# A fused attention layer on one core: conversions in pairs, key pages loaded sooner, 2 KB stores, and ScalarE's order and scans

## The chip, the core and the metric

One NeuronCore of a Trainium2 chip runs the whole program. TensorE (PE) multiplies and transposes, VectorE (DVE), ScalarE (ACT) and GpSimd (POOL) do the element work, and SyncE (SP) does nothing but issue transfers. The metric is the device time of one execution in microseconds (us). Less is better.

## What is computed

The input x is 32 x 32 x 512: 32 sequences of 32 tokens with 512 features. A first layer adds to each sequence a product with a 32 x 32 matrix that is picked by an index. The second is attention with 32 query heads and 8 key heads of 128 elements, whose keys and values are partly new and partly in a cache of 64 pages of 32 tokens:

```python
x = x + einsum('bct,bcd->bdt', x, L0_weights[subjects])
q, k, v = x @ Wq.T, x @ Wk.T, x @ Wv.T            # 32, 8 and 8 heads of 128
q, k = rope(rmsnorm(q) * q_norm, pos), rope(rmsnorm(k) * k_norm, pos)
k_all = concat([k_cache[block_table], k]); v_all = concat([v_cache[block_table], v])
scores = where(valid, einsum('bqhd,bkhd->bhqk', q, repeat(k_all, 4)) * SCALE, -1e30)
out = x + einsum('bqhk,bkhd->bqhd', softmax(scores), repeat(v_all, 4)) @ Wo.T
```

## The kernel before

**Two stages.** The first is a loop over 96 *units* (`for u in range(NU)`, one such loop in each engine's program). A unit is one of 12 *chunks* of 512 columns of the projection weights (8 of the queries in units 0 to 63, 2 of the keys in 64 to 79, 2 of the values in 80 to 95) times one of 8 groups of 128 tokens. The second is a loop over 256 *steps* (`for i in range(STEPS)`), one for each sequence and key head: scores, softmax, weighting of the values, and in the later steps the output projection of earlier groups (`ps_y`). Each number is held as two parts, a high and a low one, so that three products stand for one.

**A unit.** PE makes 12 products into `ps_proj` and then turns the rotated heads of the unit three before it (`ps_rt<-fixed,roped`, L1707). ACT squares the 512 columns, writes the high part of the turned heads (`stage`, L1125) and of the next chunk's weights (`wt_hi`). DVE rotates (`rot`, L1395 for queries, L1403 for keys, four instructions), writes the low part of the turned heads (`stage`, L1413) and, in four of eight units, the low part of the next weights (`wt_lo`). POOL adds the two halves (`roped`). SP stores the turned heads to `q_t` or `k_new_t` in DRAM.

**What holds PE back in this loop.** PE may be three units ahead, since `ps_proj` has three buffers. Its transposes at the end of unit u wait for `v_rtlo`, which is DVE's L1413 of the unit five before, and DVE does that one in its own unit u-2:

```python
un = u - LAG
...
if un >= 2:
    pe.wait_ge(v_rtlo, un - 1)
```

**The tasks.** Beside the projections 84 *tasks* go over the cache pages and the weights, 0.5 MB each: 52 *scans* (largest magnitude; ACT L1137, or DVE L1423 when `scan_on_dve`) and 32 *conversions* (ACT L1145 writes the high part, then DVE L1427 the low part, then SP stores the two as `k_pages_t` or `v_pages`). `TASKS` is their fixed order, `TASK_IN[u]` says which are done in unit u: before, two in each of units 1 to 6 and one in each unit from 7 to 78. A task's data go through one of four buffers `c_nat`: SP loads task t+4 (`load_c`, L682) after it has seen task t done. The scales for the conversions come from the scans: `reduce_tops` at units `K_BOUND` and `V_BOUND`, with PE's and DVE's small steps three and six units later.

**Keys and queries for the steps.** For each sequence SP loads 16 key pages into `kt` (L719), the queries into `qt` (L706) and the new keys (L708). The pages of sequence 0 go out in units 54 to 69, those of sequence 1 from `NEXT_KEYS_AT` on, one a unit; later ones during the steps.

**A step on ACT and DVE.** ACT writes the high part of the turned probabilities (`t_hi`, L1043) and DVE the low part (`t_lo`, L1285). Once in four steps ACT also takes the context out of `ps_o` (`ot_hi_of`, L1073), and DVE its low part (`ot_lo`, L1302). From step 24 on, in just those steps, DVE does `t_lo` first of all (`late_new`).

Of the kernel before, what the change touches and what calls it, by code (L numbers as in the profile page):

```python
# [9 lines left out]
F16 = mybir.dt.float16  # L10
# [8 lines left out]
B, SEQ, HID = 32, 32, 512  # L19
D, HQ, HK = 128, 32, 8  # L20
# [9 lines left out]
GB = P // SEQ  # L30
# [29 lines left out]
def build(nc, x, rows_in, table, l0_w, wq_t, wk_t, wv_t, wo_t, norms_in, kc_t, v_cache, wv,  # L60
# [23 lines left out]
    k_pages_t = nc.dram_tensor("k_pages_t", (PAGES, D, NHALF * BLK), F16).ap()  # L84
    k_new_t = nc.dram_tensor("k_new_t", (B, D, NHALF * BLK), F16).ap()
    q_t = nc.dram_tensor("q_t", (B, D, HK * BLK), F16).ap()

# [198 lines left out]
    XSUM_BOUND = float(np.sqrt(HID)) * (1.0 + 2.0**-10)  # L286
    KEYS_AT, NEXT_KEYS_AT, PREFETCH, NEW_V_AT = 54, 80, 87, 93
    WO_LOADS = {84: 0, 86: 1, 88: 2}
# [4 lines left out]
    TOP_STEP = 3  # L293
    K_BOUND, V_BOUND, W_BOUND = 11, 47, 80

    def mixed(convs, scans):
# [3 lines left out]
        for i in range(n):  # L300
# [3 lines left out]
            else:  # L304
# [6 lines left out]
             + [("scan", n) for n in WO_SCANS[:7]] + mixed(V_CONVS, WO_SCANS[7:]))  # L311
    PAIRS = 6
    TASK_AT = 1
    TASK_OF = {what: t for t, what in enumerate(TASKS)}
    TASK_IN = {u: [] for u in range(NU)}
    for t in range(len(TASKS)):
        TASK_IN[TASK_AT + t // 2 if t < 2 * PAIRS else TASK_AT + t - PAIRS].append(t)

    def scan_on_dve(n):
        return n % 3 == 2  # L320

    def scanned(eng, n):

        if scan_on_dve(n):
            eng.wait_ge(v_scan, n // 3 + 1)
        else:
            eng.wait_ge(a_scan, n - n // 3 + 1)

# [14 lines left out]
    def wo_scanned(eng):  # L343
        eng.wait_ge(a_scan, NSCAN - NSCAN // 3)
        eng.wait_ge(v_scan, NSCAN // 3)

# [303 lines left out]
    with persist, nc.Block() as block:  # L650
        @block.sync
        def _(sp):
# [48 lines left out]
            def load_queries(b):  # L701

                s = b % 2
                if b >= 2:
                    sp.wait_ge(t_qk, HK * (b - 1))
                sp.dma_start(qt[s][:].rearrange("p j f -> p (j f)"), q_t[b]).then_inc(d_qt[s], 16)  # L706
                edge = kt[s][:].rearrange("p (a f) -> p a f", f=BLK)[:, 0:2 * NPP + 2:2 * NPP + 1, :]
                sp.dma_start(edge, k_new_t[b].rearrange("d (h f) -> d h f", h=NHALF)).then_inc(d_kt[s], 16)  # L708

# [25 lines left out]
            for u in range(NU):  # L735
# [6 lines left out]
                if LAG < u <= NN + LAG:  # L742
                    un = u - LAG - 1
                    cn, gn = units[un]
                    kind, _, k = chunks[cn]
                    sp.wait_ge(v_rtlo, un + 1)
                    at_k = k if kind == "q" else NHALF - 1 - k
                    dst = (q_t if kind == "q" else k_new_t)[GB * gn:GB * (gn + 1), :, at_k * BLK:(at_k + 1) * BLK]
                    sp.dma_start(dst.rearrange("b d f -> d b f"), stage[un % NST][:].rearrange("p (b f) -> p b f", b=GB)
                                 ).then_inc(d_st[un % NST], 16)  # L750
# [35 lines left out]
                if NEXT_KEYS_AT <= u < NEXT_KEYS_AT + NPP:  # L786
                    load_pages(1, u - NEXT_KEYS_AT, 1)
                if u in WO_LOADS:
# [210 lines left out]
        def _(act):  # L999
# [798 lines left out]
```

## Time and profile before

| | before |
|---|---|
| median of 3 executions | 999.94 us (999.54 to 1003.92) |
| the profiled execution | 1002.31 us, of which the span is 1000.5 us |
| PE busy | 960.5 us, 96% |
| DVE busy | 831.1 us, 83% |
| ACT busy | 754.4 us, 75% |
| POOL busy | 579.8 us, 58% |

The span is from the first to the last instruction of the profiled execution; 1.8 us of its time lie outside. The busy shares are means over two stages that have little in common, so the stretches are read one by one below: 54 to 304 us hold the units 7 to 80, 304 to 341 us the rest of the units up to the first scores, and 341 to 967 us the steps.

### The profile page before, as it was taken

What the parts mean: (1) busy time and instruction counts of PE and PEld (TensorE: products, weight loads), DVE (VectorE), ACT (ScalarE), POOL (GpSimd) and SP (SyncE); (2) the same over time, 40 slices, a digit from 0 to 9 for tenths busy, and PEclk for the clock granted to TensorE, in tenths of its full rate; (3) what the DMA queues carried; (4) which work ended last, traced back from release to release, by engine and by line L of the source; (5) the groups of instructions that cost most, each with busy time, mean ns of one, the idle gap of its engine ahead of it and who ended that gap; (6) DMA issues with size and microseconds to landing.
All of it is one profiled execution on the core that took longest, in us unless ns stands there. A gap on an engine that the chain in (4) does not pass through costs nothing.

```text
span 1000.5 us, 25118 instructions
## 1 busy us (share of the span) xinstructions
PE 960.5 (96%) x8075; PEld 797.7 (80%) x8075; DVE 831.1 (83%) x1844; ACT 754.4 (75%) x2104; POOL 579.8 (58%) x861
## 2 busy tenths in 40 slices
PE   6899999999899999899999999999999999999998
PEld 4578888887677787788888888888888888878885
DVE  7889999999997688888878878888887887878880
ACT  5898999988784688878777777777777777767760
POOL 5565665565893067666755655565566556655550
PEclk9999999999999999999999999999999999999999
DMA  5899999989998999999999999999999999999940
GB/s 196 298 318 323 330 383 370 384 276 389 391 335 270 337 310 360 337 290 272 292 316 269 289 310 284 278 301 280 314 259 288 335 260 276 316 296 258 264 128 11
DMA packets 249907, 294.92 MB, mean 295 GB/s; under 512 B 79024, under 2 KB 206512, under 8 KB 247216
## 3 DMA queue, kind: packets, MB, share of 16 engines
q1 hardware_dynamic: 231088, 226.07, 76.5%
q0 software_dynamic: 18688, 67.25, 18.1%
q8 instruction: 65, 1.06, 0.4%
q14 instruction: 66, 0.54, 0.2%
HBM read 231.77 MB, written 46.27 MB: 278 GB/s over the span
## 4 chain that ended last, share of the span: by engine, by line
PE 74%; DVE 12%; issue 4%; ACT 3%; DMA 3%; POOL 2%; SPq 1%; DVEq 0%; ACTq 0%; POOLq 0%
PE ps_proj L1531 17%; PE ps_y L1531 16%; PE ps_o L1612 14%; PE ps_s L1569 8%; PE ps_t L1583 7%; PE ps_s L1573 7%; PE ps_rt L1707 2%; DVE probs L1265 2%; DVE rot L1403 2%; DVE c_stage L1427 2%; DVE stage L1413 1%; PE ps_o L1624 1%; DVE wt_lo L1231 1%; DVE rot L1395 1%; DMA c_nat<-in_L_cond_k_cache 1%
## 5 line engine op out<-in xcount | busy, mean ns | idle before, releaser
L1037 ACT ACTIVATE probs<-probs,neg_max 128x544 f32<-128x544 f32 x256 | 191.7, 749 | 137.8 <-DVE neg_max L1265 130.5
L1265 DVE CUSTOM_DVE_ANT_0 probs<-ps_s,mask,row_scale 128x544 f32<-128x544 f32 x256 | 200.4, 783 | 51.4 <-PE ps_s L1573 42.9
L1612 PE MATMUL ps_o<-pt,vs 128*128 128x128 f16 x3072 | 213.9, 219 | 0.9 <-DMA vs<-v_pages,v_row 0.9
L1612 PEld LDWEIGHTS ps_o<-pt,vs 128*128 128x128 f16 x3072 | 193.3, 98 | 15.7 <-DMA vs<-v_pages,v_row 1.5
L961 POOL TENSOR_SCALAR probs<-probs,recip 128x512 f32<-128x512 f32 x144 | 99.8, 693 | 170.1 <-DVE recip L1273 167.5
L907 POOL TENSOR_TENSOR roped<-rot 128x256 f32<-128x256 f32 x160 | 144.9, 927 | 81.3 <-DVE rot L1395 76.1
L1531 PE MATMUL ps_proj<-wt_hi,x0t_hi 128*128 128x512 f32 x384 | 158.6, 414 | 6.5 <-DVE x0t_lo L1221 6.0
L1285 DVE SCALAR_TENSOR_TENSOR pt<-ps_t,pt 128x512 f16<-128x512 f32 x190 | 130.3, 686 | 41.5 <-ACT pt L1043 41.3
L1531 PE MATMUL ps_y<-wo,ot_hi 128*128 128x512 f16 x512 | 153.4, 381 | 2.4 <-DVE ot_lo L1302 2.4
L1531 PE MATMUL ps_proj<-wt_hi,x0t_lo 128*128 128x512 f32 x384 | 150.3, 393 | 0.0
L1531 PE MATMUL ps_proj<-wt_lo,x0t_hi 128*128 128x512 f32 x384 | 149.3, 390 | 0.0
L942 POOL DMA_INDIRECT vs<-v_pages,v_row x128 | 130.8, 1022 | 27.7 <-issue 12.3
L1569 PE MATMUL ps_s<-kt,qt 128*128 128x256 f16 (+1 forms) x768 | 136.6, 287 | 1.7 <-DMA kt<-k_pages_t 1.7
L1573 PE MATMUL ps_s<-kt,qt 128*128 128x288 f16 (+1 forms) x768 | 126.2, 273 | 3.5 <-DVE neg_max L1265 3.2
L1583 PE MATMUL ps_t<-fixed,probs 128*128 128x128 f32 x760 | 115.1, 274 | 5.1 <-POOL probs L961 2.4
L1043 ACT ACTIVATE pt<-ps_t 128x512 f16<-128x512 f32 x190 | 111.6, 587 | 9.2 <-PE ps_t L1583 7.3
L1583 PEld LDWEIGHTS ps_t<-fixed,probs 128*128 128x128 f32 x760 | 92.2, 141 | 32.1 <-POOL probs L955 4.5
L1112 ACT ACTIVATE squares<-ps_proj 128x128 bf16<-128x128 f32 x320 | 85.2, 296 | 24.8 <-PE ps_proj L1531 24.8
L1531 PE MATMUL ps_y<-wo,ot_lo 128*128 128x512 f16 x256 | 97.0, 379 | 0.0
L1573 PEld LDWEIGHTS ps_s<-kt,qt 128*128 128x128 f16 x768 | 74.0, 98 | 22.7 <-DVE neg_max L1265 7.4
L1531 PEld LDWEIGHTS ps_proj<-wt_hi,x0t_hi 128*128 128x128 f32 x384 | 72.2, 188 | 21.4 <-DVE x0t_lo L1221 8.2
L955 POOL TENSOR_SCALAR probs<-probs,recip 128x544 f32<-128x544 f32 (+1 forms) x64 | 43.2, 674 | 77.5 <-DVE recip L1273 75.6
(162 smaller groups left out, 1809.7 us busy)
## 6 DMA issues: line engine op xcount, KB each, us to landing
kt<-k_pages_t SPq DMA_DIRECT2D x512, 128.0 KB
c_nat<-in_L_cond_k_cache SPq DMA_DIRECT2D x32, 512.0 KB, 6.2
q_t<-stage SPq DMA_DIRECT2D x64, 256.0 KB, 7.0
c_nat<-in_L_cond_v_cache SPq DMA_DIRECT2D x32, 512.0 KB, 7.0
qt<-q_t SPq DMA_DIRECT2D x32, 512.0 KB, 3.3
w_nat<-in_L_cond_Wq SPq DMA_DIRECT2D x8, 1024.0 KB, 8.0
k_pages_t<-c_stage SPq DMA_DIRECT2D x16, 512.0 KB, 5.3
c_nat<-in_L_cond_Wo SPq DMA_DIRECT2D x16, 512.0 KB, 7.0
```

The lines of the kernel that those rows point to most:

```text
L907: last = pool.tensor_tensor(dst, a, b, ALU.add)
L942: pool.indirect_dma_start(vs[b % 2][:, c].rearrange("p j s d -> p (j s d)"), None, v_pages, bass.IndirectOffsetOnAxis(ap=v_row[:, b * NCH ...
L961: pool.tensor_scalar(old_keys(i), old_keys(i), col(recip, i), 1.0, ALU.mult, ALU.mult).then_inc(p_old, 1)
L1037: act.activation(pr, pr, ACT.Exp, bias=col(neg_max, i), scale=-1.0, accum_out=col(row_sum, i)).then_inc(a_exp, 1)
L1043: act.activation(pt_part(i, 0), t_bank("t", i)[:], ACT.Copy, scale=P_SCALE).then_inc(a_thi, 1)
L1265: dve.tensor_tensor_reduce(out=probs_of(i), in0=ps_s[:, score_cols(i):score_cols(i) + KEYS], in1=mask[(i // HK) % 2][:, mask_at(i):mask_at ...
L1285: dve.scalar_tensor_tensor(pt_part(i, 1), t_bank("t", i)[:], P_SCALE, pt_part(i, 0), ALU.mult, ALU.subtract).then_inc(v_tlo, 1)
L1531: ins = pe.matmul(ps, a, b, start=first and n == 0, stop=last and n == len(pairs) - 1)
L1569: pe.matmul(own[0], q[:, a], k[:, b, own[1]:own[2]], start=n2 == 0, stop=n2 == 2)
L1573: ins = pe.matmul(shared[0], q[:, a], k[:, b, shared[1]:shared[2]], start=n2 == 0, stop=n2 == 2)
L1583: ins = pe.transpose(t_bank("t", i)[:, c * P:(c + 1) * P], probs_of(i)[:, SEQ * (i % 2) + c * P:SEQ * (i % 2) + (c + 1) * P], ident[:])
L1612: ins = pe.matmul(ps_o[n % 2][:, jl * P:(jl + 1) * P], v[:, part, :], pt[pt_slot(i)][:, NCH * half + c, :], start=jl == 1 and c == 0 and k ...
```

## The change

Six edits, made together:

- `q_t` and `k_new_t` are laid out by group of four sequences. A unit's store is now one run of 2048 bytes in each partition where it was four of 512. The query load, which was one run of 4096 bytes, becomes eight of 512.
- Units 18, 26, 34 and 42 do two tasks each, so that every task after them comes one unit sooner for each such unit passed, and four units sooner from unit 42 on. The last task is done in unit 74 and was done in unit 78. `V_BOUND` moves from 47 to 43.
- The last two scans that DVE had (numbers 47 and 50) go to ACT.
- The key pages of sequence 1 are loaded from unit 76 on, was 80, pages 2 to 15 first and then 0 and 1, behind a wait for `v_proj` of unit 79.
- In a step ACT does `ot_hi_of` after `t_hi`, not ahead of it.
- The waits that count scans are adapted.

```diff
-    k_new_t = nc.dram_tensor("k_new_t", (B, D, NHALF * BLK), F16).ap()
-    q_t = nc.dram_tensor("q_t", (B, D, HK * BLK), F16).ap()
+    k_new_t = nc.dram_tensor("k_new_t", (NG, D, NHALF, GB * BLK), F16).ap()
+    q_t = nc.dram_tensor("q_t", (NG, D, HK, GB * BLK), F16).ap()
...
-    KEYS_AT, NEXT_KEYS_AT, PREFETCH, NEW_V_AT = 54, 80, 87, 93
+    KEYS_AT, NEXT_KEYS_AT, PREFETCH, NEW_V_AT = 54, 76, 87, 93
-    K_BOUND, V_BOUND, W_BOUND = 11, 47, 80
+    K_BOUND, V_BOUND, W_BOUND = 11, 43, 80
-    PAIRS = 6
-    TASK_AT = 1
+    PAIR_UNITS = (1, 2, 3, 4, 5, 6, 18, 26, 34, 42)
+    TASK_UNITS = [u for u in range(1, NU) for _ in range(2 if u in PAIR_UNITS else 1)]
     for t in range(len(TASKS)):
-        TASK_IN[TASK_AT + t // 2 if t < 2 * PAIRS else TASK_AT + t - PAIRS].append(t)
+        TASK_IN[TASK_UNITS[t]].append(t)
+
+    SCAN_SPLIT = NSCAN - 6
     def scan_on_dve(n):
-        return n % 3 == 2
+        return n % 3 == 2 and n < SCAN_SPLIT
...
-                sp.dma_start(qt[s][:].rearrange("p j f -> p (j f)"), q_t[b]).then_inc(d_qt[s], 16)
+                g, a = divmod(b, GB)
+                mine = slice(a * BLK, (a + 1) * BLK)
+                sp.dma_start(qt[s][:], q_t[g, :, :, mine]).then_inc(d_qt[s], 16)
...
-                    dst = (q_t if kind == "q" else k_new_t)[GB * gn:GB * (gn + 1), :, at_k * BLK:(at_k + 1) * BLK]
-                    sp.dma_start(dst.rearrange("b d f -> d b f"), stage[un % NST][:].rearrange("p (b f) -> p b f", b=GB)
+                    sp.dma_start((q_t if kind == "q" else k_new_t)[gn, :, at_k], stage[un % NST][:]
...
-                    load_pages(1, u - NEXT_KEYS_AT, 1)
+                    pg = (u - NEXT_KEYS_AT + 2) % NPP
+                    if pg == 0:
+                        sp.wait_ge(v_proj, NN)
+                    load_pages(1, pg, 1)
...
             for i in range(STEPS):
-                if at(i, OE) is not None:
-                    ot_hi_of(at(i, OE))
                 if at(i, TNE) is not None:
                     tn_hi(at(i, TNE))
                 if i < NP2 and not by_dma(i):
                     t_hi(i)
+                if at(i, OE) is not None:
+                    ot_hi_of(at(i, OE))
```

Three places in the order of the instructions. On DVE, units 74 to 77, near the end of the key chunks (`c_stage` is a conversion, `abs_sums` a scan, `rot` and `stage` the unit's own work) stood, before:

```order
L1403 SCALAR_TENSOR_TENSOR rot<-ps_proj,rstd,rope_k 128x2x128 x4
L1413 TENSOR_TENSOR stage<-ps_rt,stage 128x4x128
L1231 TENSOR_TENSOR wt_lo<-w_nat,wt_hi 128x4x128
L1427 SCALAR_TENSOR_TENSOR c_stage<-c_nat,scale,c_stage 128x8x128
L1403 SCALAR_TENSOR_TENSOR rot<-ps_proj,rstd,rope_k 128x2x128 x4
L1413 TENSOR_TENSOR stage<-ps_rt,stage 128x4x128
L1231 TENSOR_TENSOR wt_lo<-w_nat,wt_hi 128x4x128
L1423 TENSOR_REDUCE abs_sums<-c_nat 128x1
```

and in the changed kernel in units 74 and 75, as in 76 and 77 (its lines are numbered six higher):

```order
L1409 SCALAR_TENSOR_TENSOR rot<-ps_proj,rstd,rope_k 128x2x128 x4
L1419 TENSOR_TENSOR stage<-ps_rt,stage 128x4x128
L1237 TENSOR_TENSOR wt_lo<-w_nat,wt_hi 128x4x128
L1409 SCALAR_TENSOR_TENSOR rot<-ps_proj,rstd,rope_k 128x2x128 x4
L1419 TENSOR_TENSOR stage<-ps_rt,stage 128x4x128
```

So the conversions and the scan are gone from these units. The first piece shows units 75 and 76.

On DVE in units 18 and 19, at the first of the four doubled units, the changed kernel has:

```order
L1401 TENSOR_TENSOR rot<-ps_proj,rope_q 128x1024
L1419 TENSOR_TENSOR stage<-ps_rt,stage 128x4x128
L1233 SCALAR_TENSOR_TENSOR wt_lo<-w_nat,w_inv,wt_hi 128x4x128
L1433 SCALAR_TENSOR_TENSOR c_stage<-c_nat,scale,c_stage 128x8x128 x2
L1401 TENSOR_TENSOR rot<-ps_proj,rope_q 128x1024
L1419 TENSOR_TENSOR stage<-ps_rt,stage 128x4x128
L1233 SCALAR_TENSOR_TENSOR wt_lo<-w_nat,w_inv,wt_hi 128x4x128
L1429 TENSOR_REDUCE abs_sums<-c_nat 128x1
```

Before, unit 18 had one conversion, unit 19 the other, and the scan came in unit 20.

On ACT, in a step that takes the context out, before:

```order
L1037 ACTIVATE probs,row_sum<-probs,neg_max 128x544
L1073 ACTIVATE ot_hi<-ps_o 128x32x16
L1043 ACTIVATE pt<-ps_t 128x512
L1037 ACTIVATE probs,row_sum<-probs,neg_max 128x544
L1060 ACTIVATE ptn<-ps_t 32x256 x2
```

and in the changed kernel:

```order
L1043 ACTIVATE probs,row_sum<-probs,neg_max 128x544
L1049 ACTIVATE pt<-ps_t 128x512
L1079 ACTIVATE ot_hi<-ps_o 128x32x16
L1043 ACTIVATE probs,row_sum<-probs,neg_max 128x544
L1066 ACTIVATE ptn<-ps_t 32x256 x2
```

The high part of the turned probabilities (`pt`) now goes ahead of that of the context (`ot_hi`).

## Rows read from the trace of the kernel before

**Rows 1.** Busy time by stretch; (x) is the number of instructions.

```profile
core 0: us, PE busy (x) PEld busy (x) DVE busy (x) ACT busy (x) POOL busy (x), PEclk, DMA share, GB/s
57.60:239.80 182.20, 182.03 (x916) 150.11 (x915) 174.23 (x215) 164.19 (x642) 109.14 (x130) 1.00 1.00 350
239.80:275.00 35.20, 30.80 (x149) 23.68 (x148) 33.08 (x53) 26.50 (x106) 28.66 (x35) 1.00 1.05 392
275.00:303.70 28.70, 25.97 (x127) 20.55 (x126) 28.07 (x50) 21.20 (x77) 25.68 (x32) 1.00 0.89 316
340.90:412.40 71.50, 64.52 (x679) 54.44 (x679) 61.10 (x155) 59.02 (x131) 41.31 (x53) 1.00 0.98 321
412.40:950.00 537.60, 530.92 (x5468) 451.38 (x5467) 440.02 (x1184) 404.22 (x944) 322.06 (x530) 1.00 1.02 289
```

**Rows 2.** Chain that ended last, 303 to 312 us: start, us, what.

```profile
303.99 2.77 PE ps_proj L1531 x12
306.76 0.44 PE ps_rt L1707 x4
```

**Rows 3.** PE's waits, 239.8 to 303.7 us: us in total, times, longest.

```profile
PE ps_rt L1707 <- DVE stage L1413: 6.6, 8, 1.1
```

**Rows 4.** DVE in time order; first rotations of the key units 64, 73, 74, 75, 78.

```profile
248.02 1.66 DVE L1403 SCALAR_TENSOR_TENSOR rot<-ps_proj,rstd,rope_k 128x256 f32<-128x256 f32 x4 [2.12 <-ACT squares L1112]
...
277.35 1.65 DVE L1403 SCALAR_TENSOR_TENSOR rot<-ps_proj,rstd,rope_k 128x256 f32<-128x256 f32 x4
...
283.58 1.66 DVE L1403 SCALAR_TENSOR_TENSOR rot<-ps_proj,rstd,rope_k 128x256 f32<-128x256 f32 x4 [0.63 <-POOL rstd L931]
...
286.36 1.28 DVE L1427 SCALAR_TENSOR_TENSOR c_stage<-c_nat,scale,c_stage 128x1024 f16<-128x1024 f32 x1
287.55 1.65 DVE L1403 SCALAR_TENSOR_TENSOR rot<-ps_proj,rstd,rope_k 128x256 f32<-128x256 f32 x4
...
295.25 1.21 DVE L1423 TENSOR_REDUCE abs_sums<-c_nat 128x1 f32<-128x1024 f32 x1
...
300.96 1.65 DVE L1403 SCALAR_TENSOR_TENSOR rot<-ps_proj,rstd,rope_k 128x256 f32<-128x256 f32 x4
302.53 0.68 DVE L1413 TENSOR_TENSOR stage<-ps_rt,stage 128x512 f16<-128x512 f32 x1
```

**Rows 5.** DVE in time order; rotations of the query units 61, 62 and 63.

```profile
236.89 1.21 DVE L1395 TENSOR_TENSOR rot<-ps_proj,rope_q 128x1024 f32<-128x1024 f32 x1
...
241.06 1.21 DVE L1395 TENSOR_TENSOR rot<-ps_proj,rope_q 128x1024 f32<-128x1024 f32 x1
...
242.79 1.21 DVE L1395 TENSOR_TENSOR rot<-ps_proj,rope_q 128x1024 f32<-128x1024 f32 x1
```

**Rows 6.** SP's load of task 33 (conversion 6), and ACT's use of it.

```profile
118.47 0.62 SPq L682 DMA_DIRECT2D c_nat<-in_L_cond_k_cache  x1
...
129.00 1.17 ACT L1145 ACTIVATE c_stage<-c_nat,scale 128x1024 f16<-128x1024 f32 x1
```

**Rows 7.** Transfers of task loads (57 to 304 us) and conversions on DVE: ns min/median/max.

```profile
L1427 DVE SCALAR_TENSOR_TENSOR c_stage<-c_nat,scale,c_stage x32: 1267/1749/1776, 97.4 to 299.3; 128x1024 f16<-128x1024 f32 x32
...
DMA to landing us min/median/max: 3.6/6.7/11.6
```

**Rows 8.** Waits, 412.4 to 950 us: us in total, times, longest.

```profile
DVE pt L1285 <- ACT pt L1043: 38.2, 57, 2.3
...
PE ps_y L1531 <- DVE ot_lo L1302: 1.7, 6, 0.3
```

**Rows 9.** The first key load that PE waited for in the steps.

```profile
376.86 0.50 PE L1569 MATMUL ps_s<-kt,qt 128*128 128x256 f16 x3 [0.93 <-DMA kt<-k_pages_t]
```

More of the change, by code:

```diff
@@ L326, in scanned @@
         else:
-            eng.wait_ge(a_scan, n - n // 3 + 1)
+            eng.wait_ge(a_scan, n - min(n, SCAN_SPLIT) // 3 + 1)
     NQ = NG * HK
@@ L343, in wo_scanned @@
     def wo_scanned(eng):
-        eng.wait_ge(a_scan, NSCAN - NSCAN // 3)
-        eng.wait_ge(v_scan, NSCAN // 3)
+        eng.wait_ge(a_scan, NSCAN - SCAN_SPLIT // 3)
+        eng.wait_ge(v_scan, SCAN_SPLIT // 3)
     TOPS = {K_BOUND: (0, ((0, 0, NKCH),), k_scanned),
@@ L705, in load_queries @@
                     sp.wait_ge(t_qk, HK * (b - 1))
-                sp.dma_start(qt[s][:].rearrange("p j f -> p (j f)"), q_t[b]).then_inc(d_qt[s], 16)
+                g, a = divmod(b, GB)
+                mine = slice(a * BLK, (a + 1) * BLK)
+                sp.dma_start(qt[s][:], q_t[g, :, :, mine]).then_inc(d_qt[s], 16)
                 edge = kt[s][:].rearrange("p (a f) -> p a f", f=BLK)[:, 0:2 * NPP + 2:2 * NPP + 1, :]
-                sp.dma_start(edge, k_new_t[b].rearrange("d (h f) -> d h f", h=NHALF)).then_inc(d_kt[s], 16)
+                sp.dma_start(edge, k_new_t[g, :, :, mine]).then_inc(d_kt[s], 16)
             def load_pages(b, first, count):
```

## The prediction

> **What bounds the kernel now.** I read the busy time by stretch first [rows 1]. In 57.6 to 239.8 us, units 8 to 63, PE is busy for 182.03 of 182.20 us, so that nothing can be won there and only something lost. In 239.8 to 303.7 us (units 64 to 80, the key chunks) PE is busy for 30.80 + 25.97 = 56.77 of 63.90 us: 7.1 us of idle time, 4.4 in the first part and 2.7 in the second, while DVE has 33.08 and 28.07 of them, 96%. In the first steps, 340.9 to 412.4 us, PE idles for 7.0 us. In the steps from 412.4 to 950 us it idles for 6.7 of 537.6, and that is more than half of the kernel with no more than that to give. So the change has some 7 us to win in the key units and a few in the first steps; everywhere else it can only lose.
>
> The chain gives PE's own pace: 2.76 us of products and 0.44 us of transposes, 3.20 us a unit [rows 2]. In 239.8 to 275 us PE issues 149 instructions, at 16 a unit 9.3 units, whose own pace is 29.8 us: 5.4 lost. In 275 to 303.7 it is 127, 7.9 units, 25.4 us: 3.3 lost [rows 1]. Who holds PE is told by its waits: eight transposes waited for DVE's L1413, 6.6 us in all and 1.1 at most [rows 3]. That is the rule of the code: DVE may start its unit at most two units of PE, 6.4 us, less its own rotation and L1413 after PE's products. Those two take 1.73 us for queries (241.06 to 242.79) [rows 5] and 2.25 for keys (300.96 to 303.21) [rows 4], so that the *lag* of DVE behind PE may be 4.7 us in a query unit and 4.2 in a key unit. Beyond that PE stalls for the rest.
>
> **The change part by part.** The ledger of the lag: each unit adds what DVE does in it and takes 3.20 away.
>
> *The second half of the key units.* DVE runs from 283.58 to 300.96 us without a pause, 17.38 us for units 74 to 77, or 4.35 each [rows 4]. The lag grows by 4 x 1.15 = 4.6 us and PE loses the 3.3 us of this part. The change takes from these four units the conversions of 74, 75 and 77 (1.2 us as 286.36 to 287.55, up to 1.7) [rows 4, 7] and the scan of 76 (295.25 to the next rotation, 1.1): 1.2 + 1.7 + 1.1 + 1.7 = 5.7. Left are 11.7 us, 2.9 a unit, under 3.20: the lag shrinks, and no stall is left. Unit 73 gets a conversion (1.2), which leaves the lag near 3.5, still allowed. **-3.3 us** (bounds 2.7, the idle time alone, and 3.5). ACT takes the two scans at 1.1 us each (ACT is busy for 47.7 of 63.9 us there [rows 1]), which hides them.
>
> *The first half.* Units 64 to 72 take DVE 277.35 - 248.02 = 29.3 us up to unit 73, against 9 x 3.2 = 28.8 for PE, but it comes in late: rot of unit 64 waited 2.12 us more [rows 4], at the change from query to key units, where the rotation needs a factor that POOL makes after its additions. Before, these units hold six conversions and one scan; after, six conversions. It saves 1.1, and in exchange the lag at its start is greater, since units 60 to 62 hold two conversions where they held two, but from a higher start. I take 0.8 of the 5.4 as saved. **-0.8 us.** Bounds: 0 and 2.5.
>
> *The doubled units and what follows.* A conversion beside `wt_lo` makes a query unit 4.17 us long (236.89 to 241.06) [rows 5]. A second one adds 1.27 to 1.75 [rows 7], so unit 18 comes to 5.5 to 5.9 us and puts 2.3 to 2.7 on the lag at one stroke. The lag starts from 1.2 there, and the units 19 to 21 (3.6, 4.2, 2.5 us) carry it to about 4.8: a stall of 0.2 to 0.6. The same sum at 26, 34 and 42 peaks at 4.2, 4.1 and 3.3 (0 to 0.2 us of stall). In units 49 to 53 the key tables (two instructions in each of units 49 and 50) now meet conversions 16 to 18, which began at unit 54 before: peak 5.3, stalls of 0.1 and 0.6. Units 60 to 62 give 0.2. Together **+1.4 us**; bounds 0.5 and 2.5. DVE's pauses in this stretch were 182.20 - 174.23 = 8.0 us [rows 1], and the two conversions that move in cost 3.4, so it holds on average.
>
> *Less time for the loads.* A load goes out when the task four before is done. Task 33 was loaded at 118.47 and used at 129.00 us, 10.5 us later [rows 6]; it is now the second of unit 26, with three units instead of four between, so 7.3 us. The median landing is 6.7, the longest 11.6 [rows 7]. This holds for four tasks at each of the four places: ACT will wait for some, 0 to 2 us. What hides it is DVE's own lag of 3 to 4 us just there. At nothing; if the cover fails, it is the slower rival below.
>
> *The stores.* 80 stores go from 512 to 128 runs, 32 query loads from 128 to 1024: 30,720 fewer and 28,672 more. In the units this helps the landings that the last paragraph is about; in the steps it puts the query load, which goes ahead of the pages, up to 0.4 us behind. PE waited 0.93 us for pages of sequence 2 [rows 9]. Nearest rows say +0 to +1 us, I take **+0.5**.
>
> *ACT's order in the steps.* DVE waited 38.2 us for ACT's `pt`, 57 times, 0.67 each [rows 8]. With `t_hi` first, L1285 comes up to 0.5 us sooner in the step where DVE has it first. But PE is busy for 530.92 of 537.6 us whatever DVE does, and of its 6.7 only the 1.7 that it waited for `ot_lo` [rows 8] lie near. `ot_lo` comes later on DVE than masked_max, so that `ot_hi` 0.5 us later is covered. Before step 24 DVE does `ot_lo` ahead of `t_lo`, and there up to 0.5 us in five steps can be lost. **-0.5 us**, bounds -2 and +2.
>
> *Key pages sooner, `V_BOUND`, SP's waits.* Pages of sequence 1 are wanted only when the eight heads of sequence 0 are through; nothing waits for them. The wait for `v_proj` of unit 79 at unit 90 is long met; behind it on SP stand stores of v. SP's wait for all conversions moves to unit 76, three units after the last, and may hold SP for some 4 us; behind it are stores from eight buffers, which have eight units of 3.2 us. Nothing.
>
> **The sum.** -3.3 - 0.8 + 1.4 + 0.5 - 0.5 = -2.7 us. The profiled execution took 1002.31 us (span 1000.5 and 1.8 around it): 999.6. It lies 2.4 above the median of 999.94, and I take that distance as it is: **997.2 us**.
>
> **A rule against it.** In 239.8 to 275 us the transfers moved 392 GB/s [rows 1]. The change brings four loads of 0.5 MB and two stores into the stretch up to 239.8: 182.2 us x 350 GB/s = 63.8 MB become 66.9. At 392 GB/s that needs 171 us, so there is room. The Trainium skill, page "DMA: Bandwidth & Descriptors", section "Specifications", gives some 358 GB/s as the limit of one core at its memory; by that the 66.9 MB would need 187 us, an estimate of 4.7 us more for the stretch. The trace does not agree: 392 stood for 35 us.
>
> **The rivals.**
> - *Less is saved than is lost in the doubled units* (no change). If second conversions cost 1.75, the lag enters unit 64 a microsecond higher, and the first half gives 1 us back: -3.3 + 2.5 + 1 + 0.5 - 0.5 = +0.2, about 1000 us. For it: DVE is at 96% from unit 8 on. Against: the ledger of before gives 8 us of stalls, near what is there.
> - *DVE catches up entirely* (faster). All 7.1 us of the key units go, and ACT's order wins 1 to 2 in the steps: 999.94 - 8.5 = 991.5 us. For it: the scans leave DVE and the lag allowed is nearly met in several places. Against it: the pause at unit 64 stays.
> - *The loads come late* (slower). Its place is the doubled units: if landings rise above 7.3 us under the denser transfers, ACT waits, its squares are late and DVE's lag passes 4.7. If no more than the 350 GB/s of this stretch can be had, 66.9 MB take 191 us, 8.9 more: 999.94 + 8.9 - 2.7 = 1006 us. It decides from landings of about 9 us on (7.3 and what the lag covers). For it: the median is 6.7 and the longest 11.6 us. Against: 392 GB/s were moved, and the stores have fewer runs.
>
> **The numbers.** A measurement of this kernel tells about 0.5%, 5 us, from no change, whose bounds are 994.9 and 1004.9. Forecast 0.52 (994.5 to 999.5), no change 0.19, catching up 0.19, late loads 0.10. Faster by over 0.5%: the third and a part of the first, 0.24. Slower: the last and little else, 0.11. The rest, 0.65, is within. Range 990 to 1003 us: it takes in the first three and leaves out the last.
>
> **What would show it.** Right: in units 74 to 80 no transpose waits for L1413; PE's idle time in the key units falls from 7.1 to about 3.5, in the first half alone; up to unit 63 it rises from 0.2 to 1 or 2, at units 20 to 23 and 51 to 56; the steps' length stays. Wrong: ACT's waits for `c_nat` in the units 26 to 48, or a step loop that is shorter by more than 2 us, or waits for `kt` in it.

## The result, and the profile after

The changed kernel takes 1005.9 us (median of 22 executions, 999.8 to 1010.0) where the kernel before took 1001.4 in executions on the same chips (22, 999.5 to 1004.1). The ratio is 1.0034, with a 95% interval of 1.0021 to 1.0047: by the ratio some 3.4 us slower (the two medians lie 4.5 apart), on the other side of the forecast. The profiled execution took 1007.41 us, with a span of 1005.6.

The busy time by stretch, the same stretches of the program as in [rows 1], with the same columns:

```profile
core 0: us, PE busy (x) PEld busy (x) DVE busy (x) ACT busy (x) POOL busy (x), PEclk, DMA share, GB/s
58.30:250.40 192.10, 186.59 (x918) 150.88 (x916) 178.21 (x218) 168.24 (x648) 108.67 (x130) 0.99 0.96 350
250.40:287.10 36.70, 33.22 (x161) 26.07 (x161) 33.22 (x55) 28.97 (x111) 31.25 (x39) 1.00 1.03 404
287.10:313.20 26.10, 25.77 (x131) 21.09 (x129) 24.06 (x50) 16.73 (x73) 22.63 (x32) 1.00 0.64 224
347.10:419.70 72.60, 64.42 (x679) 54.37 (x679) 61.06 (x155) 59.13 (x131) 40.91 (x53) 1.00 0.97 311
419.70:954.60 534.90, 528.66 (x5463) 449.82 (x5462) 439.63 (x1183) 408.32 (x944) 321.42 (x529) 1.00 1.04 292
```

Units 8 to 63 took 182.2 us and now take 192.1. That is the whole loss and more. Behind it the key units and the later steps are a little faster, and the first steps took 1.1 us longer. Every kernel below is read in such stretches, so here they are for all of them, worked out from the trace: from the start of PE's first product of unit 7 to that of unit 64, and so on, and then from the first scores of step 0 to those of steps 32 and 248 (us, one profiled execution each; "rest" is from unit 82 to the first scores).

| kernel | 7 to 64 | 64 to 74 | 74 to 82 | rest | steps 0 to 32 | 32 to 248 |
|---|---|---|---|---|---|---|
| before | 185.4 | 38.0 | 29.1 | 34.0 | 71.5 | 537.0 |
| changed | 195.3 | 36.7 | 26.1 | 34.0 | 72.6 | 534.8 |
| e1, changed, five buffers | 189.0 | 36.7 | 26.1 | 34.0 | 72.1 | 534.6 |
| e2, changed, no doubled units | 185.4 | 35.9 | 28.4 | 33.9 | 72.1 | 534.9 |
| e3, before, doubled units | 192.1 | 37.6 | 27.2 | 34.0 | 70.6 | 536.9 |
| e4, before, five buffers | 185.5 | 37.8 | 29.2 | 34.0 | 71.1 | 537.3 |
| e5, before, 2 KB layouts | 185.4 | 38.0 | 29.2 | 34.0 | 74.2 | 535.8 |
| e6, before, ScalarE's order | 185.7 | 37.9 | 29.3 | 34.0 | 73.4 | 533.1 |
| e7, other doubled units, five | 189.5 | 36.8 | 25.6 | 34.0 | 72.3 | 534.4 |
| e8, the same with four | 193.1 | 38.6 | 25.6 | 34.0 | 72.6 | 534.3 |
| e9, order, four scans | 185.4 | 35.9 | 29.3 | 34.0 | 70.7 | 534.1 |
| e10, two scans | 185.5 | 37.0 | 28.3 | 34.0 | 71.8 | 537.3 |
| e11, doubled units later, five | 187.1 | 37.2 | 25.6 | 34.0 | 71.8 | 534.8 |
| e12, the best | 187.2 | 36.2 | 25.6 | 34.0 | 72.1 | 534.6 |

What the last two columns hold by chance of one execution: the granted clock fell to one half for 3.4 us at 395 us in e5 and at 397 in e6, in the first steps, and at 889 to 897 us in before, e1, e3, e4, e7, e8, e10, e11 and e12, where the steps 225 and 226 together take 1.1 to 1.4 us more than in the other five. In the changed kernel and e2 step 37 takes 1.3 and 1.5 us more than in before, with a wait of PE for values (`vs`).

**The loss.** Waits of the changed kernel in 58.3 to 250.4 us (us in total, times, longest):

```profile
DVE rot L1401 <- ACT squares L1118: 12.5, 14, 1.9
...
ACT c_nat L1143 <- DMA c_nat<-in_L_cond_Wo: 3.8, 2, 3.6
PE ps_rt L1713 <- DVE stage L1419: 3.0, 7, 0.8
...
PE ps_l L1558 <- ACT angle L1011: 2.4, 2, 1.6
ACT c_nat L1143 <- DMA c_nat<-in_L_cond_v_cache: 1.5, 1, 1.5
```

DVE's wait for ACT's squares was 6.2 us (8 times) before and is 12.5 (14 times). ACT waits for task data, in two large pieces. And PE waits in two ways, of which the prediction knew only one. The time line shows how the pieces hang together (start, duration, what; in brackets the idle time before it and what ended it):

```profile
117.04 0.56 SPq L665 DMA_DIRECT2D w_nat<-in_L_cond_Wq  x1
...
119.61 0.86 SPq L684 DMA_DIRECT2D c_nat<-in_L_cond_v_cache  x1
...
129.08 1.06 ACT L1143 ACTIVATE c_nat<-c_nat 128x1024 f32<-128x1024 f32 x1 [1.50 <-DMA c_nat<-in_L_cond_v_cache]
...
131.29 1.22 DVE L1401 TENSOR_TENSOR rot<-ps_proj,rope_q 128x1024 f32<-128x1024 f32 x1 [1.01 <-ACT squares L1118]
...
138.84 1.23 DVE L1401 TENSOR_TENSOR rot<-ps_proj,rope_q 128x1024 f32<-128x1024 f32 x1 [0.79 <-ACT squares L1118]
...
143.12 0.39 PE L1558 MATMUL ps_l<-w_sq,ones_p 128*128 128x4 f32 x2 [1.56 <-ACT angle L1011]
...
145.07 0.63 PE L1537 MATMUL ps_proj<-wt_hi,x0t_hi 128*128 128x512 f32 x1
...
176.40 0.64 SPq L684 DMA_DIRECT2D c_nat<-in_L_cond_Wo  x1
...
186.02 1.06 ACT L1143 ACTIVATE c_nat<-c_nat 128x1024 f32<-128x1024 f32 x1 [3.56 <-DMA c_nat<-in_L_cond_Wo]
...
199.03 0.39 PE L1558 MATMUL ps_l<-w_sq,ones_p 128*128 128x4 f32 x2 [0.80 <-ACT angle L1011]
```

Unit 27 is the first behind a doubled one. Its task (34) was loaded at 119.61 us, 2.57 us behind the load of the next weights (`w_nat`, 1 MB), and landed 9.5 us later. ACT wanted it 8.0 us after the issue and stood for 1.50. ACT has no slack to work that off in the units 28 and 29, since it makes the next weights there; in the units 29 to 31 it stays 3.2 to 3.7 us behind PE, DVE waits for its squares again and again, and DVE's lag goes to 5.5 us. At unit 32 PE stands for 1.56 us for something that the prediction doesn't name: `ps_l`, the sum of the squared weights of the next chunk, which ACT makes beside the weights (L1011). The same happens behind the doubled unit 42: task 52 was loaded at 176.40, landed 9.6 us later and cost ACT 3.56; PE stood at `ps_l` for 0.80 at unit 48.

Not all that PE lost there was waiting. The granted clock (the column before the last two):

```profile
141.60:144.80 3.20, 1.68 (x8) 1.42 (x9) 3.20 (x4) 3.20 (x17) 0.94 (x2) 0.96 0.89 331
144.80:148.20 3.40, 3.40 (x13) 2.65 (x11) 3.40 (x5) 1.15 (x4) 1.98 (x3) 0.53 1.00 288
148.20:151.00 2.80, 2.80 (x15) 2.27 (x14) 2.15 (x3) 2.34 (x10) 2.63 (x5) 1.00 1.06 376
```

Unit 31 had lost 0.8 us and PE had stood for 1.56 us at the end of unit 32; behind that the clock was at about one half, 1.2 GHz, for the 3.4 us of the second row. A product took 0.63 us as in the row at 145.07, in place of 0.39, and the next started 0.43 us behind it in place of 0.23; unit 33 took 4.80 us instead of 3.20. That is 1.6 us of loss in a unit in which PE waited for nothing. The Trainium skill, page "TensorE: Matmul & The Clock Gate", section "Part 1: The HAM clock gate (the "warmup" mystery)", says that the clock has these two levels and is set by how busy the engine has been; the trace agrees in the levels (1.00 and, in the second row, 0.53) and in that PE had just waited for 1.56 us.

By unit, against the kernel before: units 31 to 33 lose 4.2 us, units 46 to 49 3.2 (less 0.4 at unit 53, where a step of `V_BOUND` stood before that is now at unit 49), unit 23 0.9 (less 0.3 at unit 24), units 54 to 56 1.9 and unit 63 0.7. With 0.1 less at unit 40 and 0.1 less in all the others this makes 10.0, the 9.9 us of the table but for rounding.

**What came true.** DVE in the units 74 and 75 of the changed kernel and at the start of unit 76, in time order, where [rows 4] had a conversion or a scan in each of the units 74 to 77:

```profile
293.57 1.65 DVE L1409 SCALAR_TENSOR_TENSOR rot<-ps_proj,rstd,rope_k 128x256 f32<-128x256 f32 x4
295.15 0.68 DVE L1419 TENSOR_TENSOR stage<-ps_rt,stage 128x512 f16<-128x512 f32 x1
295.74 0.68 DVE L1237 TENSOR_TENSOR wt_lo<-w_nat,wt_hi 128x512 fp32r<-128x512 f32 x1
296.47 1.66 DVE L1409 SCALAR_TENSOR_TENSOR rot<-ps_proj,rstd,rope_k 128x256 f32<-128x256 f32 x4
...
299.68 1.66 DVE L1409 SCALAR_TENSOR_TENSOR rot<-ps_proj,rstd,rope_k 128x256 f32<-128x256 f32 x4 [0.35 <-POOL rstd L937]
```

A unit is 2.9 us long and DVE even waits. PE's waits for DVE fell from 6.6 us [rows 3] to 3.3 in 250.4 to 287.1 us (first row) and 0.3 in 287.1 to 313.2 (second):

```profile
PE ps_rt L1713 <- DVE stage L1419: 3.3, 3, 1.5
...
PE ps_rt L1713 <- DVE stage L1419: 0.3, 1, 0.3
```

In the first steps PE's wait for key pages, 0.93 us at one place in [rows 9] and 1.7 in all before, was 2.4 (first row), and in the later steps DVE's wait for `pt`, 38.2 us in [rows 8], was 23.3 (second row):

```profile
PE ps_s L1575 <- DMA kt<-k_pages_t: 2.4, 1, 2.4
...
DVE pt L1291 <- ACT pt L1049: 23.3, 41, 1.0
```

And the landings of the task loads in the units 7 to 82, which were 3.6, 6.7 and 11.6 us in [rows 7]:

```profile
DMA to landing us min/median/max: 3.2/6.5/11.5
```

The transfers did not get slower. What was taken away is the time that they had.

### The profile page after: what moved, and what is told of

Read it like the earlier page. It is cut to its first block, busy times and chain, and to the rows that moved or that the text cites. A ratio compares the mean times of both kernels' runs of the same rounds, so it can differ in the third digit from the quotient of the medians.

```text
span 1005.6 us, 25120 instructions
## 1 busy us (share of the span) xinstructions
PE 962.4 (96%) x8075; PEld 798.1 (79%) x8075; DVE 828.1 (82%) x1842; ACT 760.8 (76%) x2108; POOL 575.6 (57%) x861
## 4 chain that ended last, share of the span: by engine, by line
PE 62%; DVE 15%; issue 6%; POOL 4%; DMA 4%; SPq 4%; ACT 3%; DVEq 0%; ACTq 0%; POOLq 0%
PE ps_y L1537 15%; PE ps_o L1618 13%; PE ps_proj L1537 9%; PE ps_s L1575 7%; PE ps_t L1589 7%; PE ps_s L1579 7%; DVE rot L1401 3%; DVE c_stage L1433 3%; DVE stage L1419 2%; SPq L723 2%; POOL vs L948 1%; DVE rot L1409 1%; DVE wt_lo L1233 1%; PE ps_o L1630 1%; ACT squares L1118 1%
## 5 line engine op out<-in xcount | busy, mean ns | idle before, releaser
L913 POOL TENSOR_TENSOR roped<-rot 128x256 f32<-128x256 f32 x160 | 142.7, 913 | 88.5 <-DVE rot L1401 87.4
L1401 DVE TENSOR_TENSOR rot<-ps_proj,rope_q 128x1024 f32<-128x1024 f32 x64 | 77.8, 1216 | 12.9 <-ACT squares L1118 12.5
```

What stands on the lines that cost most here:

```text
L913: last = pool.tensor_tensor(dst, a, b, ALU.add)
L1401: dve.tensor_tensor(rot[u % NRT][:], ps_proj[u % NPJ][:].rearrange("p (a j d) -> p a j d", a=1, j=HPC) .to_broadcast((P, 2, HPC, D)), rope ...
```

## The experiments

Twelve kernels, each timed in five rounds against the kernel before on the same chip. The ratio is to the kernel before, with its 95% interval. These intervals reach 1.0 to 2.1 us to either side, so that a difference between two of the kernels is known to some 2 us.

**e1: is it the loads?** One more buffer lets each load go out one task sooner.

```diff
-    NCN = 4
+    NCN = 5
```

> The changed kernel with five buffers c_nat in place of four, so that a load goes out one task sooner. Late loads (my theory): the two waits of ACT for c_nat after the doubled units 26 and 42 (1.5 and 3.6 us) vanish, and with them the stretches in which PE lost 4.1 us (units 31 to 33) and 3.3 us (units 46 to 49). 1005.9 - 7.4 = 998.5 us, a ratio to the kernel before of 0.997 where the changed kernel has 1.0034. Rival, DVE has too much work in and behind the doubled units whatever the loads do: ratio stays at 1.003 to 1.004, with the stalls in the same units and no wait of ACT for c_nat. Rival, the memory can't move it sooner: the landings lengthen by as much as the loads go out sooner, the waits stay and the ratio too.

Measured: 0.9999 (0.9986 to 1.0011). Its waits in the units 8 to 63, of ACT and of PE: ACT has one row left, and it is no load, and PE has less than half of what it had.

```profile
ACT squares L1118 <- PE ps_proj L1537: 16.5, 18, 1.8
...
PE ps_rt L1713 <- DVE stage L1419: 1.5, 4, 0.5
PE ps_l L1558 <- ACT angle L1011: 0.8, 1, 0.8
```

The transfers of its task loads, in the units 7 to 82:

```profile
DMA to landing us min/median/max: 3.4/7.0/11.7
```

Late loads cost 3.5 us of the changed kernel's time by the ratios (1.0034 to 0.9999), and 6.3 us by the two profiled executions (195.3 to 189.0), one of which had the fallen clock. I had put 7.4 on it: units 7 to 64 are still 3.6 us longer than before. The third rival, that the memory can't deliver sooner, falls: the stretch moved 362 GB/s where the changed kernel moved 350.

**e2: all but the doubled units.**

```diff
-    PAIR_UNITS = (1, 2, 3, 4, 5, 6, 18, 26, 34, 42)
+    PAIR_UNITS = (1, 2, 3, 4, 5, 6)
-    K_BOUND, V_BOUND, W_BOUND = 11, 43, 80
+    K_BOUND, V_BOUND, W_BOUND = 11, 47, 80
-    KEYS_AT, NEXT_KEYS_AT, PREFETCH, NEW_V_AT = 54, 76, 87, 93
+    KEYS_AT, NEXT_KEYS_AT, PREFETCH, NEW_V_AT = 54, 80, 87, 93
```

> The changed kernel with single tasks in units 18, 26, 34 and 42, bounds at unit 47 and key pages of sequence 1 from unit 80, as before; stores, ScalarE's order and the two scans stay changed. Late loads by the doubling: the whole loss is gone, and the gain at the last key units mostly too (two scans off DVE save 1 us there): ratio 0.998 to 1.000. Rival, the loss comes from the other edits (2 KB stores and 512-byte query loads, ScalarE's order): ratio 1.003 or more.

Measured: 0.9979 (0.9967 to 0.9990). Without the doubled units the change would have been a gain of 2.1 us; with them it is a loss of 3.4. They cost 5.5, and the sooner loads of key pages, taken back here too, are within this number.

**e3: the doubled units alone**, `PAIR_UNITS` and `V_BOUND` of the change put into the kernel before.

> The kernel before with two tasks in units 18, 26, 34 and 42 and bounds at unit 43, nothing else. Late loads by the doubling: +7.4 us in units 26 to 49, +1.2 in units 50 to 56, -3 in units 74 to 80: ratio 1.004 to 1.006. Rival, the loss comes from the other edits: ratio 0.996 to 1.000.

Measured: 1.0067 (1.0049 to 1.0084). The two readings agree, 5.5 and 6.7 us. The other edits are not the cause. Its trace has three pauses at `ps_l` (2.7 us in all, at units 32, 40 and 48), where the changed kernel has two, and no fall of the clock behind them.

**e4: five buffers in the kernel before.**

> The kernel before with five buffers c_nat in place of four. There the tasks of units 60 to 72 already have no time to spare: data land 8 to 10 us after the issue, just as ACT comes to them. Late loads cost also before: in units 64 to 73 PE gets back 2 to 4 us of the 5.4 that it lost, ratio 0.996 to 0.998. Rival, DVE's own work sets units 64 to 73 and the waits of ACT are hidden: ratio 0.999 to 1.001.

Measured: 0.9996 (0.9982 to 1.0009). The rival was right. Before the change ACT's waits for loads in the units 60 to 72 were hidden, and units 64 to 74 took 37.8 us against 38.0. The fifth buffer is worth something only where the doubled units have used up the time.

**e5: the 2 KB layouts alone**, in the kernel before (the two `dram_tensor` lines, the store, and the two loads of the change's diff).

> The kernel before with the 2 KB stores and the 512-byte query and key loads alone. In the profiled executions, the first steps (from the first scores to those of step 32) took 71.5 us before and 72.6, 72.0 and 72.1 in the three kernels with these layouts, but 70.6 and 71.1 in two without. Theory: the query loads, eight times as many runs, go ahead of the pages and cost 0.5 to 1 us in these steps, and nothing else moves: ratio 1.000 to 1.001. Rival: the stores with fewer runs let the task loads land sooner and ScalarE's waits in units 60 to 72 shrink: ratio 0.998. Rival: this edit is behind the 2 us that the later steps gained in all kernels that had it: ratio 0.998, and the steps 32 to 248 at 535 us, not 537.

Measured: 1.0017 (1.0007 to 1.0028), a loss of 1.7 us, with nothing moved in the units. Both rivals fall with the ratio; the 535.8 us of the later steps, near what the second named, is a trace in which the clock did not fall at 895 us, and it still has the waits that e6 takes away. Of the profiled executions the seven with this layout took 72.5 us for the steps 0 to 32 on average, the seven without it 71.6 (72.2 and 71.3 without the two in which the clock fell there). The difference lies where PE waits for key pages in these steps: 1.5 to 2.6 us with the layout, 2.1 on average, and 0 to 2.1 without it, 1.1 on average. That is 0.9 us of the loss; the rest stays open.

**e6: ScalarE's order in a step alone**, in the kernel before.

```diff
-                if at(i, OE) is not None:
-                    ot_hi_of(at(i, OE))
                 if at(i, TNE) is not None:
                     tn_hi(at(i, TNE))
                 if i < NP2 and not by_dma(i):
                     t_hi(i)
+                if at(i, OE) is not None:
+                    ot_hi_of(at(i, OE))
```

> The kernel before with ScalarE's order in a step alone (t_hi ahead of ot_hi_of). From the scores of step 32 to those of step 248 it took 537.0, 536.9 and 537.3 us in three profiles without this edit and 534.9, 534.7 and 534.9 in three with it. Theory: the order wins these 2.2 us: ratio 0.998. Rival: the gain is that of the other layout of queries and keys, and this kernel's steps stay at 537: ratio 1.000.

Measured: 0.9981 (0.9968 to 0.9994), a gain of 1.9 us. What went away is a wait that I had not listed. PE's waits in the steps from 32 on, in the kernel before:

```profile
PE ps_t L1583 <- POOL probs L961: 2.4, 1, 2.4
PE ps_s L1573 <- DVE neg_max L1265: 1.8, 4, 0.4
```

And in this one:

```profile
PE ps_t L1583 <- POOL probs L961: 2.4, 1, 2.4
PE ps_y L1531 <- DVE ot_lo L1302: 2.0, 7, 0.3
```

PE waited four times for `neg_max`, which DVE makes of a step's scores (L1265), and no longer does. Step 99 took 2.88 us before and 2.40 here, and so it is in each of the blocks of eight steps that begin at 96, 128, 160 and 192. All fourteen traces agree: the four steps (99, 131, 163 and 195) take 2.85 to 2.88 us in the five kernels with the old order, and 2.37 to 2.40 in the nine with the new one, but for single values of 2.6 in e1, e2, e9 and e12. With step 35, which is 0.3 shorter too, this makes 2.1 us on average. The rest of the 3.9 by which e6 differs from before in the last column is mostly the clock's fall at 895 us. I read it so that with `t_hi` first DVE has `t_lo` behind it sooner and comes to the scores in time; that this is the way was not tried.

**e7 and e8: doubled units where there is slack.** Two scans share a unit each time; e8 has four buffers, e7 five.

```diff
-    PAIR_UNITS = (1, 2, 3, 4, 5, 6, 18, 26, 34, 42)
+    PAIR_UNITS = (1, 2, 3, 4, 5, 6, 7, 9, 47, 49)
-    ... V_SCANS[:7]] + mixed(K_CONVS, V_SCANS[7:])
+    ... V_SCANS[:9]] + mixed(K_CONVS, V_SCANS[9:])
-    ... WO_SCANS[:7]] + mixed(V_CONVS, WO_SCANS[7:])
+    ... WO_SCANS[:9]] + mixed(V_CONVS, WO_SCANS[9:])
-    SCAN_SPLIT = NSCAN - 6
+    SCAN_SPLIT = NSCAN - 12
```

> The changed kernel with five buffers and with the four doubled units at 7, 9, 47 and 49 in place of 18, 26, 34 and 42, where both tasks are scans; two scans of the v cache go ahead of the conversions and two of Wo likewise, scans 41 and 44 go to ScalarE, bounds at unit 45. Theory: what five buffers left of the loss (units 7 to 63 took 189.1 us against 185.4 before) is that VectorE's work between units 18 and 42 comes to more than 3.2 us a unit when four more tasks fall there, and that ScalarE is late with the sums of squared weights that TensorE wants at units 24, 32 and 40. A ledger of the lag gives 247 us from unit 7 to unit 82, where it was 252.6 before and 251.8 with five buffers: ratio 0.994 to 0.996. Rival: any second task in a unit costs, wherever it lies: ratio 0.998 to 1.000, as with five buffers alone (0.9999) less the two scans.

> The same with four buffers c_nat. Theory: behind the doubled units 7, 9, 47 and 49 loads are a unit shorter of time just as they were behind 26 and 42, but there VectorE has little to do (scans alone), so a wait of ScalarE of 1 to 3 us is made up for: within 0.001 of the kernel with five buffers, less what the waits in units 60 to 70 cost (0 to 2 us). Rival: late loads cost as much here as at units 26 and 42: 4 to 6 us more than with five buffers, ratio 0.999 to 1.001.

Measured: e7 0.9981 (0.9968 to 0.9994), e8 1.0028 (1.0013 to 1.0043). For e8 the theory was wrong and the rival right: 4.7 us for one buffer less. In e8 ACT stood for 4.3 us before the task of unit 11, and DVE, idle for 5.3 us behind it, came into the work of unit 13 (the page tables) with a lag of 6.2 and had 9.2 at unit 14: slack that lies ahead of a late load hides nothing. In e7 the units 18 to 63 were nearly clean, as the ledger wanted, but units 16 and 17 took 2.6 and 1.6 us more than before. ACT's waits of e7 in 71 to 95 us:

```profile
ACT angle L1011 <- DMA w_nat<-in_L_cond_Wq: 1.3, 1, 1.3
ACT c_nat L1143 <- DMA c_nat<-in_L_cond_v_cache: 0.6, 1, 0.6
```

And its busy time behind unit 16, with the granted clock in the column before the last two:

```profile
87.50:90.10 2.60, 0.56 (x6) 0.60 (x6) 2.53 (x6) 2.60 (x13) 1.23 (x2) 1.00 0.98 380
90.10:92.00 1.90, 1.90 (x9) 1.52 (x8) 1.90 (x4) 0.78 (x4) 1.15 (x3) 0.67 0.96 325
92.00:94.70 2.70, 2.70 (x10) 2.08 (x9) 2.70 (x4) 0.00 (x0) 2.16 (x4) 0.60 1.02 322
```

With two more loads in units 7 and 9 the weights came 1.3 us late, ACT was late, DVE's lag was 6.9 us at unit 14, PE paused for 2.4, and the clock fell to one half behind the pause, as it had in the changed kernel. That the two loads delayed the weights is read from the order of events; no run tried it alone.

**e9 and e10: the scans.** e10 puts scans 47 and 50 on ACT and does nothing else; e9 takes four scans (41 too, and 44), ScalarE's order and five buffers.

```diff
+    SCAN_SPLIT = NSCAN - 12
     def scan_on_dve(n):
-        return n % 3 == 2
+        return n % 3 == 2 and n < SCAN_SPLIT
```

> The kernel before with scans 47 and 50 on ScalarE and nothing else. Theory: units 64 to 82 go from 67.1 us to some 64.3, as they did in the kernel without doubled units, so that this edit alone brings what the prediction put down to the shift of the tasks: -2.3 to -2.9 us, ratio 0.997 to 0.998. Rival: the key units gain only together with something else: ratio 0.999 to 1.000.

> The kernel before with ScalarE's order in a step, five buffers c_nat, and scans 41, 44, 47 and 50 on ScalarE; no doubled unit, no other layout. Theory, the edits add up: the order alone gave 0.9981, and taking scans off VectorE is what gives back the key units, -2.9 us for two of them and by the ledger of the lag 0.5 more for four: -1.9 - 3.4 = -5.3 us, ratio 0.9947. Rival: ScalarE's waits and its own work in units 52 to 72 make up for it, and no more than the order's share is seen: 0.998.

Measured: e10 0.9980 (0.9970 to 0.9990), e9 0.9961 (0.9946 to 0.9976). The two scans are worth 2.0 us alone. The single edits add up: -1.9 (order), +1.7 (layouts) and -2.0 (scans) make -2.2, and e2, which has all three, measured -2.1. The key pages loaded sooner were never run alone: with the 6.7 of e3 the single edits make +4.5 where the whole change measured +3.4, so that what is left for them is less than the noise. The two further scans and the fifth buffer of e9 show nothing: -1.9 and -2.0 are its -3.9 already, short of the -5.3 that I had expected.

**e11: the doubled units five units later** (the last one four), with `V_BOUND` at 44 and one more scan of Wo ahead of the conversions of v.

```diff
-    PAIR_UNITS = (1, 2, 3, 4, 5, 6, 18, 26, 34, 42)
+    PAIR_UNITS = (1, 2, 3, 4, 5, 6, 23, 31, 39, 46)
-    NCN = 4
+    NCN = 5
```

> The changed kernel with five buffers and its doubled units at 23, 31, 39 and 46 in place of 18, 26, 34 and 42 (bounds at unit 44, one more scan ahead of the conversions of v). In these units neither VectorE nor ScalarE has a part of the next weights to do. Theory: what five buffers left of the loss was in the place of the doubled units: units 7 to 64 took 189.0 us with five buffers, 185.4 before; now 185.5 to 187, and ScalarE's sums of squared weights are in time at unit 32. Ratio 0.9975 to 0.9985 (0.9999 with the old places). Rival: the work of four tasks more in units 18 to 43 is too much for VectorE wherever they lie, since it has no idle time there: still 189 us, ratio 1.000.

Measured: 0.9968 (0.9954 to 0.9982), 3.1 us better than with the old places (e1), and better than the theory asked. Units 18, 26, 34 and 42 are each the first of four in which ACT and DVE make the next weights; 23, 31, 39 and 46 come behind these. Its busy time in the units 8 to 63 and 64 to 73:

```profile
58.20:242.10 183.90, 182.69 (x916) 149.95 (x915) 177.69 (x217) 168.94 (x651) 112.60 (x130) 1.00 0.97 362
242.10:279.30 37.20, 33.51 (x163) 25.96 (x162) 35.09 (x57) 29.40 (x110) 31.39 (x39) 1.00 1.04 407
```

The pauses at `ps_l` are gone. All that PE still waited for in units 8 to 63:

```profile
PE ps_rt L1713 <- DVE stage L1419: 1.2, 2, 1.0
```

**e12: the best of it together.** The kernel before with ScalarE's order, four scans on ACT, five buffers, the doubled units of e11, and `K_TABLE_AT` at 46.

> The best that the runs so far point to: the kernel before with ScalarE's order, five buffers, four scans on ScalarE, doubled units at 23, 31, 39 and 46, and the key tables three units sooner (46 and 47), without the 2 KB layouts. Theory: order -1.9, units 7 to 82 in 247 us by the ledger of the lag, where they took 252.5 before: -7.4 us, ratio 0.9926. Rival: units 18 to 43 lose with the doubled units what the key units win, as in the changed kernel, and it comes out at or above the kernel without doubled units and with four scans on ScalarE (0.9947 expected).

Measured: 0.9943 (0.9923 to 0.9964), 996.72 us: 5.7 us faster than before and 9.1 faster than the changed kernel by the ratios. It fell short of the expected 0.9926, which lies just inside the interval. The trace has units 7 to 82 at 249.0 us instead of 247 and says where: unit 48 took 5.31 us, 1.9 more than before. The weights were 1.2 us late for ACT at unit 44, as in e7, and the key tables, put at units 46 and 47, met the doubled unit 46, so that ACT and DVE were both late there. PE's waits in the units 8 to 80:

```profile
PE ps_rt L1709 <- DVE stage L1415: 2.6, 3, 1.5
PE ps_l L1554 <- ACT angle L1007: 1.6, 1, 1.6
```

Against e9 at 0.9961 the doubled units bring 1.8 us at their best, and the intervals of the two overlap: that they bring anything is not shown.

## Why the prediction was wrong, step by step

- *Second half of the key units, -3.3.* Right: 29.1 us became 26.1, and no transpose waited for more than 0.3 us. The scans alone bring 0.8 of it (e10), the shift the rest.
- *First half, -0.8.* 38.0 became 36.7, -1.3, in the bounds.
- *Doubled units and what follows, +1.4, bounds 0.5 and 2.5.* Too small. With the loads out of the way (e1) units 7 to 64 were 3.6 us longer than before. The ledger was DVE's alone: it had unit 18 at 5.5 to 5.9 us (5.4) and a peak of 5.3 in units 49 to 53 (5.7 in e1, 6.2 in the changed kernel). Its other peaks were right (4.8, 4.2, 4.1 and 3.3 us behind the four doubled units; 4.8, 3.9, 4.1 and 3.3 in e1). What it lacked is ACT's own lag of 1 to 2 us in the four units behind a doubled one, and so the pause at `ps_l` at unit 32, where ACT holds PE directly: 1.0 of the 3.6 us. Its stalls were too small too: 1.4 us at the units 54 to 56 and 0.7 at 63, where it had 0.7 and 0.2. e11 moved the doubled units away from the weights and got back 1.9 of the 3.6 us in the trace, and 3.1 us by the ratios.
- *"Less time for the loads ... What hides it is DVE's own lag of 3 to 4 us just there. At nothing".* This is the step that failed: what it put at nothing cost 3.5 us (the changed kernel against e1, by the ratios), with ACT standing for 1.5 and 3.6 us. Its arithmetic was right: 7.3 us of time, and "it decides from landings of about 9 us on"; the two loads took 9.5 and 9.6. Two things in it were wrong. It weighed 7.3 against the median of 6.7, though 16 loads had to go through four such places and the first load behind the doubled units 26 and 42 goes out just behind 1 MB of weights; the five task loads that went out within 3 us behind such a load in the units 10 to 59 took 8.6 to 11.5 us, so that there the long landings are the rule. And it took DVE's lag as a cover for a wait of ACT. A lag covers a wait of the engine that is ahead of it only if that engine can catch up; ACT is busy for 90% of these units [rows 1], and DVE, which is busy for 96%, must not idle at all. What DVE waited for squares went on its lag, and what passed the allowed 4.7 us went on to PE.
- *Stores +0.5, ACT's order -0.5.* Measured +1.7 and -1.9, of which the first is above its bound of +1 and the second inside. Both had their signs. The order's gain was looked for at `ot_lo` (1.7 us before, 2.0 in e6); it was at the wait of PE for `neg_max`, four times 0.4 us.
- *The scans.* Costed inside the key units, where e10 confirms them: -2.0.
- *The slower rival* had 0.10 and came with 1006 us. It named place and mechanism, and its limit of 9 us. Its price was reached by a sum that does not hold: that no more than 350 GB/s can be had. The stretch again shows 350 GB/s (67.2 MB in 192.1 us), but with the same work e1 moved 362, e12 364, and units 64 to 74 of e11 407. The loss is made of waits, not of a ceiling; that 8.9 lies so near the 9.9 of the trace is chance. So is the 1006 us in part: it stands on a median of 999.94 from three executions, and 22 have 1001.4. The Trainium skill's 358 GB/s (page "DMA: Bandwidth & Descriptors", section "Specifications") was passed in the last three of these.
- *The signs.* Two of those named for being wrong came: ACT's waits for `c_nat` behind the units 26 and 42 (1.5 and 3.6 us), and PE's wait for `kt` (2.4). PE's idle time up to unit 63 was 5.5 us, not 1 or 2.
- *The sum.* By the ratios: order -1.9, layouts +1.7, scans -2.0, and the doubled units +5.5 with their gain at the end of the key units already taken off. Of the 5.5, 3.5 are late loads (e1) and 3.1 the place of the doubled units (e11), so that the shift itself, well placed and fed, comes out at -1.1 (e11 less e2), which is within the noise.

## What to carry to other kernels

When a task is moved up and its buffers are not, take the time that its load then has and set it against the longest landings at that very place, among them those behind a large load of another kind, and never against the median. A lag of an engine further down is no cover: it covers only if every engine between can catch up, so write the ledger for each engine that hands work to the next, and look for the places at which an early engine holds the last one directly. Where the work of a unit rises and falls, put extra work behind its heavy part and give it one buffer more.

## What the runs showed of the hardware

- **A pause of PE can cost as much again as it lasts.** In the changed kernel a loss of 0.8 us in unit 31 and a pause of 1.6 at the end of unit 32 were followed by 3.4 us at a granted clock of 0.53 (1.2 GHz for nearly all of it), and in e7 and e8 a pause of 2.4 us likewise; unit 33 lost 1.6 us by it and unit 17 of e7 1.6.
- **The same pause is followed by a fall of the clock or not.** All fourteen kernels have a pause of 2.4 us between 886 and 900 us, where PE waits for POOL's `probs`. At its end or just behind it the clock fell to one half for 3.4 us in nine of them, and it did not in the changed kernel, e2, e5, e6 and e9. Waits for key pages near 400 us do the same: a fall in e5 (2.4 us) and e6 (2.1), none in the changed kernel (2.4), e7 (2.2) and e8 (2.3). The kernel before, and then the changed one:

```profile
893.46 0.66 PE L1583 MATMUL ps_t<-fixed,probs 128*128 128x128 f32 x4 [2.42 <-POOL probs L961]
...
894.70:898.10 3.40, 3.40 (x24) 2.68 (x23) 2.15 (x5) 0.95 (x4) 2.21 (x5) 0.50 1.02 364
```

```profile
899.79 0.66 PE L1589 MATMUL ps_t<-fixed,probs 128*128 128x128 f32 x4 [2.42 <-POOL probs L967]
...
900.00:903.40 3.40, 3.29 (x41) 2.73 (x39) 2.12 (x6) 1.69 (x3) 2.80 (x5) 1.00 0.91 280
```

  Pauses of 1.5 and 1.6 us in e3 and e12 were not followed by a fall either. So a fall, and what it costs, can't be told from the length of the pause alone, and what else decides the traces don't tell.
- **The start of a kernel scatters.** The first product of unit 7 came between 53.2 and 56.7 us in the fourteen profiled executions, with nearly the same program up to there; this alone is 3.5 us of the spread between executions, and single profiled executions of such kernels can't be compared by their totals, only by their stretches.
- **Loads of one size land after very different times.** A 0.5 MB load landed after 3.2 to 11.7 us. In the kernel before, those with at most two other transfers under way at their issue took 4.9 us on average (7 of 70), those with five or more 8.1 (39); in the changed kernel it is 6.7 and 8.1. With a fifth buffer the median rose (6.5 to 7.0 us, 7.9 in e11) while ACT waited for none of them in the units 8 to 63.
